# Three lanes on one core: row norms moved to ScalarE, FP4 rescales to GpSimd, two banks for the scan's B rows, and 1,876 unread identity products on TensorE

## The reference

```
x = x + 0.5 * ffn(layernorm(x))      # FP4 quantize/dequantize in blocks of 16, silu-gated, 352 wide
x = x + mamba(layernorm(x))          # 2 layers; each: rmsnorm, in_proj, conv of 4 taps, silu,
                                     # selective scan over 16 states, gate, out_proj
x = x + 0.5 * ffn(layernorm(x))      # the same FP4 ffn
x = x + 0.5 * moe(layernorm(x))      # 8 dense experts 128 -> 512 -> 128, sigmoid gates over 0.5
x = x + attention(layernorm(x))      # its own inner layernorm, 16 heads of 8, relative bias, causal
x = x + 0.5 * moe(layernorm(x))
```

## Time and profile before

| | before |
|---|---|
| median of 3 runs | 2972.98 us (2966.27 to 2973.26) |
| the profiled execution: its time, its span | 2990.37 us, 2988.6 us |
| TensorE busy | 2550.3 us (85%) |
| VectorE busy | 2134.1 us (71%) |
| ScalarE busy | 1498.5 us (50%) |
| GpSimd busy | 1255.3 us (42%) |
| mean granted TensorE clock | 0.836 of full speed |

### The profile page before, as it was taken

How to read it: one execution, slowest core, us unless ns; L and a number is a source line. 1 busy time by engine, 2 the same in 40 slices (tenths; PEclk the granted TensorE clock), 3 DMA queues, 4 the chain that set the end, 5 groups by cost and what they waited for, 6 DMA issues and landing times.

```text
span 2988.6 us, 34443 instructions
## 1 busy us (share of the span) xinstructions
PE 2550.3 (85%) x11161; PEld 1535.6 (51%) x11161; DVE 2134.1 (71%) x4265; ACT 1498.5 (50%) x2989; POOL 1255.3 (42%) x1050
## 2 busy tenths in 40 slices
PE   3667656886899797998999899979899999999898
PEld 2121122443357553665557565746566566567675
DVE  6878899889885778557586988788786866652420
ACT  1432332543374453545466447655665557456554
POOL 1537546473653154352442554535272454510111
PEclk9565566896696896679988899979899999899899
DMA  4213212121221011210110112111020112100000
GB/s 141 78 53 95 73 58 79 49 81 49 64 78 36 19 56 48 60 54 19 52 52 29 58 32 67 47 54 60 26 89 24 45 54 65 50 4 1 1 4 4
DMA packets 88544, 150.12 MB, mean 50 GB/s; under 512 B 10565, under 2 KB 21485, under 8 KB 88110
## 3 DMA queue, kind: packets, MB, share of 16 engines
q1 hardware_dynamic: 88366, 147.94, 15.9%
HBM read 145.26 MB, written 2.65 MB: 49 GB/s over the span
## 4 chain that ended last, share of the span: by engine, by line
PE 65%; DVE 23%; ACT 6%; issue 4%; POOL 2%; DVEq 0%; DMA 0%; SPq 0%; POOLq 0%; ACTq 0%
PE c_bank L861 16%; PE c_bank L869 16%; DVE hst L658 8%; PE a_bank L709 6%; DVE a_bank L652 4%; PE b_bank L1023 4%; PE a_bank L699 3%; PE b_bank L1012 3%; PE b_bank L1036 2%; PE b_bank L1035 2%; PE a_bank L680 2%; PE b_bank L539 1%; PE b_bank L520 1%; PE b_bank L1034 1%; PE a_bank L715 1%
## 5 line engine op out<-in xcount | busy, mean ns | idle before, releaser
L778 POOL TENSOR_TENSOR prod_c<-hst,prod_c 128x512 f32<-128x512 f32 x512 | 662.6, 1295 | 716.7 <-DVE hst L658 710.7
L658 DVE TENSOR_TENSOR_SCAN hst<-dA,a_bank 128x512 f32<-128x512 f32 x512 | 623.4, 1218 | 21.1 <-ACT dA L767 7.9
L861 PE MATMUL c_bank<-c_xT,w 128*128 128x512 f32 x1024 | 565.1, 658 | 15.0 <-ACT hid L893 8.4
L767 ACT ACTIVATE dA<-delta,a_neg 128x510 f32<-128x510 f32 x512 | 364.6, 718 | 360.5 <-DVE hst L658 355.9
L869 PE MATMUL c_bank<-w,hid 128*128 128x128 f32 x4096 | 537.0, 282 | 0.0
L869 PEld LDWEIGHTS c_bank<-w,hid 128*128 128x128 f32 x4096 | 497.5, 195 | 66.8 <-issue 37.5
L893 ACT ACTIVATE hid<-c_bank,b 128x512 f32<-128x512 f32 x512 | 350.0, 687 | 193.0 <-PE c_bank L861 190.9
L652 DVE TENSOR_TENSOR a_bank<-du,a_bank 128x512 f32<-128x512 f32 x512 | 354.9, 693 | 126.0 <-PE a_bank L699 98.2
L917 POOL TENSOR_TENSOR xs<-xs,weighted_y 128x512 f32<-128x512 f32 x128 | 168.0, 1313 | 643.2 <-ACT weighted_y L901 642.7
L709 PE MATMUL a_bank<-prod_c,ident 128*128 128x512 f32 x512 | 389.0, 851 | 26.8 <-POOL prod_c L783 18.6
L699 PE MATMUL a_bank<-bc,sel 64*128 64x512 bf16 x512 | 244.5, 477 | 170.7 <-DVE a_bank L652 159.6
(11 more groups left out here) (168 smaller groups left out, 3387.1 us busy)
## 6 DMA issues: line engine op xcount, KB each, us to landing
prod_c<-c_rows SPq DMA_DIRECT2D x512, 256.0 KB, 3.2
w<-in_w SPq DMA_DIRECT2D x2, 2048.0 KB
xs<-in_x SPq DMA_DIRECT2D x8, 256.0 KB, 8.2
bias<-skew SPq DMA_DIRECT2D x1, 2048.0 KB, 8.6
out_dram<-xs SPq DMA_DIRECT2D x8, 256.0 KB, 2.3
in_wT<-in_in_wT SPq DMA_DIRECT2D x1, 512.0 KB
c_rows<-bcC SPq DMA_DIRECT2D x16, 32.0 KB, 1.6
b_hq<-in_w_gu SPq DMA_DIRECT2D x1, 384.0 KB, 3.2
```

The source lines that it names most:

```text
L658: nc.vector.tensor_tensor_scan(hst[:, s % RS, :], dA[:, s % RA, :], S.bank[0][:, :], 0.0, ALU.mult, ALU.add).then_inc(M.h.sem, 1)
L767: nc.scalar.activation(half_batches(dA[:, s % RA, :], 1), half_batches(delta[:, h, :], 1), ACT.Exp, scale=a_neg[:, l, h, n:n + 1]).then_in ...
L778: nc.gpsimd.tensor_tensor(prod[:, s % RP, :], hst[:, s % RS, :], cring[:, s % RC, :], ALU.mult).then_inc(M.pp.sem, 1)
L861: nc.tensor.matmul(S.bank[up_bank(e, c)][:, :], w1[:, e, c * 128:(c + 1) * 128], S.xT[:, :], start=True, stop=True).then_inc(M.up.sem, 1)
```

## The change

It has four parts, and the order strings of all engines are new.

1. **Norms.** `normed_dve` is gone. `normed_act` applies every norm on ACT, in four activations of 128x128 with `rstd` as scale and a new `shift` (minus mean times rstd) as bias. POOL makes `shift` in two further 128x4 instructions. The rms norm of a mamba layer takes its squares on ACT (`squares_act`, with an accumulating output) in place of `bn_stats`, `bn_aggr` and two small DVE instructions. The adds `x + hm` and `x + x1` go from DVE to POOL.
2. **Rescale.** In the ffn the last instruction of the quantize chain goes to POOL (`rescale_pool`): per ffn one of 128x512 and two of 128x704.
3. **B rows.** The B row of an even step goes to bank 2, that of an odd step to bank 0; DVE multiplies in place and scans the same bank. The row of step s now waits for the scan of step s-2 in place of the multiply of step s-1.
4. **Identity products.** `warm_pe` (letter `d` in `ORDER_PE`) multiplies the identity by itself, 128x128 in float32, into bank 0 of lane c, which nobody reads. It waits once per gap between passes, until the last weighted output of the pass before has left the bank; while a pass is under way (from its transposes to its last `down` product) the string has no `d`. It holds 1,876 of them: 1,086 ahead of pass 0 (layers 0 to 2 of lane a), 381 between passes 0 and 1, 193 between 1 and 2, and 216 between the others up to pass 13.

```
-        def normed_dve(dve, L, S, x, dst, rstd, done, rms=False):
-            dve.wait_ge(rstd.sem, L.at(rstd, 1))
+        def normed_act(act, L, S, x, dst, rstd, done, rms=False):
+            act.wait_ge(rstd.sem, L.at(rstd, 1))
             for t in range(TT):
                 if rms:
-                    ins = nc.vector.tensor_scalar(dst[:, t, :], x[:, t, :], S.rstd[:, t:t + 1], None, ALU.mult)
+                    ins = nc.scalar.activation(dst[:, t, :], x[:, t, :], ACT.Copy, scale=S.rstd[:, t:t + 1])
                 else:
-                    ins = nc.vector.tensor_scalar(dst[:, t, :], x[:, t, :], S.mv[:, t, 0:1], S.rstd[:, t:t + 1],
-                                                  ALU.subtract, ALU.mult)
+                    ins = nc.scalar.activation(dst[:, t, :], x[:, t, :], ACT.Identity, scale=S.rstd[:, t:t + 1],
+                                               bias=S.shift[:, t:t + 1])
...
+        def rescale_pool(pool, L, dst, n, qs, q, made, rounded, k):
+            nb = n // BLK
+            pool.wait_ge(rounded.sem, L.at(rounded, k))
+            nc.gpsimd.tensor_tensor(dst.rearrange("p (b s) -> p b s", s=BLK), q[0][:, 0:n].rearrange("p (b s) -> p b s", s=BLK),
+                                    qs[:, 0, 0:nb].unsqueeze(2).to_broadcast([128, nb, BLK]), ALU.mult).then_inc(made.sem, 1)
             yield
...
-                if s:
-                    dve.wait_ge(M.h.sem, L.at(M.h, s))
-                nc.vector.tensor_tensor(S.bank[0][:, :], du[:, h, :], S.bank[2][:, :], ALU.mult).then_inc(M.dBx.sem, 1)
+                b_bank = S.bank[2 - s % 2 * 2][:, :]
+                nc.vector.tensor_tensor(b_bank, du[:, h, :], b_bank, ALU.mult).then_inc(M.dBx.sem, 1)
...
-                    if s:
-                        pe.wait_ge(M.dBx.sem, L.at(M.dBx, s))
-                    nc.tensor.matmul(S.bank[2][:, :], sel[64:128, s % NST, :], bc3[64:128, :],
+                    if s == 1:
+                        pe.wait_ge(M.delta.sem, L.at(M.delta, 1))
+                    elif s:
+                        pe.wait_ge(M.h.sem, L.at(M.h, s - 1))
+                    nc.tensor.matmul(S.bank[2 - s % 2 * 2][:, :], sel[64:128, s % NST, :], bc3[64:128, :],
...
+        def warm_pe(pe, L):
+
+            waited = 0
+            pe.wait_ge(s_wf, 16 * len(load_f))
+            while True:
+                assert L.passes is not None
+                if waited < L.passes:
+                    waited = L.passes
+                    pe.wait_ge(moe.wy.sem, moe.wy.per * waited)
+                nc.tensor.matmul(sc_.bank[0][:, 0:128], ident[:, :], ident[:, :], start=True, stop=True)
+                yield
```

More of the change, by code:

```diff
@@ L105, with merge @@
 ORDER_SP = (
-    "a246c2a65caca51ca66ca50ca49c3")
-def merge(order, lanes):
+    "a240caca70c2a76ca50ca58ca33c3")
+def merge(order, lanes, spare=None):
     i = 0
     while i < len(order):
-        lane = lanes[ord(order[i]) - ord("a")]
+        lane = spare if order[i] == "d" else lanes[ord(order[i]) - ord("a")]
         j = i + 1
@@ L341, in __init__ @@
                 self.proj = sig(n + "_out_product", 1, use, uses)
+                self.added = sig(n + "_added", 1, use, uses)
         class MoeS:
@@ L406, in stats_dve @@
                 ins = nc.vector.bn_aggr(S.mv[:, t, :], S.stats[:, t, :])
-                if t == TT - 1 and not rms:
+                if t == TT - 1:
                     ins.then_inc(done.sem, 1)
@@ new lines, in rstd_pool, with squares_act @@
+            yield
+        def squares_act(act, L, S, x, done):
+            for t in range(TT):
+                ins = nc.scalar.activation(S.xn[:, t, :], x[:, t, :], ACT.Square, accum_out=S.mv[:, t, 1:2])
+                if t == TT - 1:
+                    ins.then_inc(done.sem, 1)
+                else:
+                    ins.then_inc(L.sem, L.one())
+                yield
+        def normed_act(act, L, S, x, dst, rstd, done, rms=False):
+            act.wait_ge(rstd.sem, L.at(rstd, 1))
@@ L667, in mamba_dve @@
             nc.vector.tensor_tensor(hm[:, :, :], hm[:, :, :], S.bank[0][:, :].rearrange("p (t d) -> p t d", d=D),
-                                    ALU.add).then_inc(L.sem, L.one())
+                                    ALU.add).then_inc(M.added.sem, 1)
             yield
-            dve.wait_ge(L.sem, L.n)
         def mamba_pe(pe, L, S, M, l):
@@ L830, in moe_pe @@
             N = M.norm
+            L.passes = None
             pe.wait_ge(N.out.sem, L.at(N.out, 1))
@@ L1143, in a_pool @@
                 L.g = g
-                yield from rstd_pool(pool, L, sa, mam_ln[0], mam_ln[1])
+                yield from rstd_pool(pool, L, sa, mam_ln.stats, mam_ln.rstd)
                 for l in range(LAYERS):
                     yield from mamba_pool(pool, L, sa, mam[l], l, g * LAYERS + l)
+                last = mam[LAYERS - 1].added
+                pool.wait_ge(last.sem, L.at(last, 1))
+                nc.gpsimd.tensor_tensor(x_of(g), x_of(g), hm[:, :, :], ALU.add).then_inc(first_done.sem, 1)
+                yield
         def a_sp(sp, L):
@@ L1266, in c_pe @@
                 yield from moe_pe(pe, L, sc_, moe)
+        def warm_pe(pe, L):
[7 more added lines that the diff above has]
+                nc.tensor.matmul(sc_.bank[0][:, 0:128], ident[:, :], ident[:, :], start=True, stop=True)
+                yield
         def c_act(act, L):
             act.wait_ge(s_wc, 16 * len(load_c))
-            for i in range(len(moe_order)):
+            for i, (second, g) in enumerate(moe_order):
                 L.g = i
-                yield from moe_act(act, L, sc_, moe)
+                yield from moe_act(act, L, sc_, moe, x_of(g))
         def c_pool(pool, L):
```

257 lines of the change are left out of this document (147 added, 110 removed).

## The result

The changed kernel takes **2876.5 us**, the median of 4 runs (2874.22 to 2881.22), against 2973.12 for the kernel before (4 runs, 2966.27 to 2989.48). The ratio is 0.9669, 95% interval 0.9624 to 0.9714. The forecast was 2847 us with a range of 2740 to 2965. On a second chip and with more runs the ratio was 0.9692 (0.9651 to 0.9734). The traced execution of the kernel before (2990 us) lies 17 us above its median here and 34 above that on the chip of the first experiments, so stretches read from it are about 1% long.

What follows compares the result with a forecast made beforehand. DVE's scans were taken to bound the kernel from 60 to 420 us and PE from 1184 us on, with both mattering between. 678 + 1854 + 92 + 240 = 2864 us of span, scaled to 2847 us, range 2740 to 2965.

Steps and rivals of the forecast that it cites:

- Place one: Start of layer 3 in lane a, where pass 0's first `up` product stands in the new order: 422 us.
- 20 + 133 = 153 us: PE's work at full speed up to 420 us in the kernel before, to which 244 us of identity products were added.
- The 25 us of idle time: PE idle time added up to the start of layer 3, since PE can't start before its first weights are quantized.
- Place two: Near the start of layer 5, where pass 1's first `up` product stands: 678 us, from 150 work, 86 products, 20 idle.
- The rest: From layer 5 to the end: 1854 us of work, 92 of identity products, 240 of overhead.
- open term: How much of some 320 us of overhead inside the passes goes; 110 us idle and 130 by the clock were taken to stay.
- main case: Gaps filled and overhead inside the passes down to 240 us: 2864 us of span, 2847 scaled; chance 0.40.
- first rival: Only the gaps are filled, idle time and clock inside the passes stay at 320 us: 2944, 2927 scaled; chance 0.27.
- three reasons: For less overhead inside the passes: two banks for the B row, some 170 us off DVE, passes entered at full clock.
- The scaling: The 2864 us span was lowered to 2847 because the profiled execution was 0.6% over the median.
- the clock does not rise: Rival: identity products don't raise the clock and cost 0.45 us each: some 3330 us; chance 0.03.
- Lane a gains nothing, but lane c is ahead: At layer 5 lane a stands as now, while pass 0 begins some 110 us earlier and pass 1 about 100.

Runs made afterwards that it cites:

- no_d: The changed kernel with all identity products taken out of PE's order: 2928.5 us, 0.9908 of the kernel before.
- late_d: The changed kernel with only the 409 identity products behind pass 1 kept: 2882.9 us, 0.9747 of the kernel before.
- half_d: The changed kernel with every second identity product left out over the whole order, 938 kept: 2851.7 us, 0.9641 of the kernel before.
- half_early: The changed kernel with 734 of the 1,467 identity products up to pass 1 kept, and all 409 behind it: 2866.5 us, 0.9633 of the kernel before.
- d32: The changed kernel with all 1,876 identity products cut from 128 to 32 columns: 3331.6 us, 1.119 of the kernel before.

## Why the prediction was right, step by step

**Place one.** 422 predicted, 436 measured. By the rows the changed kernel does 415.49 x 0.99 = 411 us of work up to layer 3 and no_d 259.18 x 0.66 = 171. Both need a correction that the prediction's "20 + 133 = 153 us" needs too. The row of the first 60 us gives a clock of 1.00, but the records there have the length of the lower level, and the clock rises only in the second of these (kernel before):

```profile
56.65 2.77 PE L539 MATMUL b_bank<-w_dnT,ffn_buf 128*128 128x128 f32 x12
...
59.85 1.82 PE L539 MATMUL b_bank<-w_dnT,ffn_buf 128*128 128x128 f32 x12
```

Twelve records of the same product take 1.50 us at the full clock (L582 at 55.73 us, changed kernel). So the first 20 us of busy time are about 10 of work, and the prediction's 153 was 143. With the same correction (the lower level up to 21 us in the changed kernel, up to 51 in no_d) the two kernels do 408 and 163 us of work. The difference over 1,086 products is 0.226 us each, priced at 0.225: the price held. The 25 us of idle time came out as 28 (20 idle, 8 by the clock). Mis-sized was the other work: 163 us, not 153. no_d has 548 records ahead of that place where the kernel before has 468; 24 of the 80 more are the transposes and gate products of pass 0, the other 56 products of the ffn in lane b, which now also stand ahead of it.

**Place two.** 678 predicted, 694 measured, of which 14 are from place one. Between the two 258 us were measured, 256 predicted.

**The rest.** 1854 + 92 = 1946 us of work predicted; 2066.91 x 0.94 = 1943 measured. Overhead 240 predicted, "110 us idle and 130 by the clock"; measured 114 and 124. This open term, which separated the main case from the first rival, came out as taken. Against the kernel before it fell by some 220 us. By the table of passes and gaps the fall has the parts that the prediction gave it. The gaps gave up 87 us of idle time and 52 of the clock's, where 86 and 55 stood; the passes 5 and 67, where 10 and 70 stood. The fall in the gaps is the products': no_d loses as much in them as the kernel before (266 and 262 us). The fall in the passes is not, since no_d has it too. So of the three reasons that the prediction gave for it the third, that PE enters each pass at the full clock, is not seen: the clock takes 60 us of the passes in no_d and 53 in late_d. Two banks and the lighter DVE are left, with the new order; the runs don't separate them.

What was wrong are the amounts that this was to be taken from. The prediction had 141 us in the gaps, all of them to go, and 320 inside the passes. Counted from the first `up` product to the last `down` product, the passes held 164 and the gaps 262, and 123 of these are still there. The two errors cancel in the sum, and that they do is luck. (From no_d to late_d the products give back 41 us of idle time and 104 of the clock's, another split than that against the kernel before: no_d has less idle time in the gaps, 116 us in place of 158, and loses more there by the clock, 150 in place of 104.)

**The scaling.** The span was 2864 predicted and 2875 measured. I scaled it down by 0.6%, because the profiled execution of the kernel before was that much above its median. The changed kernel's profiled execution was at its median (2876.84 against 2876.5). 17 of the 29 us between 2847 and 2876.5 are this step.

**What the text said would show.** L912 at about 430 and 690 us: 439 and 696. Busy times near 1960, 1630, 1380: 1946, 1606, 1371. The clock above 0.95 up to the first pass: 0.99; near 0.9 later: 0.94. L1338 was busy 483 us, where 420 stood: its records overlap, and it was the spacing that was priced. Pass 3, where the prediction found a stretch at 0.50 with PE busy throughout, still has one:

```profile
1175.00:1200.00 25.00, 25.00 (x68) 14.14 (x66) 12.15 (x29) 11.59 (x24) 10.90 (x10) 0.50 0.17 53
```

The whole pass has a clock of 0.89 in the changed kernel (1077 to 1235 us) and in no_d (1104 to 1262), and 0.77 before (1184 to 1375): the products did not mend it. The activations of the norms took 0.483 us, not 0.368, and the wide rescales on POOL 1.416, not 1.78.

**A reading.** Against "the clock does not rise" the prediction set L709's 2.07 us for two records beside its mean of 0.85 for one. A single record of L709 takes 1.06 to 1.22 us at the lower level and 0.59 at the full one, so a mean of 0.85 puts about half of its run at the full clock, not most. The conclusion stands: the records of L709 had both lengths.

**What was not foreseen.** "Lane a gains nothing, but lane c is ahead" was taken as if the earlier start were a gain of itself, and no_d shows it isn't much of one: 0.9908 with it, 0.9909 for two banks without it. That DVE's wait for the B row would rise: it is 128.8 us in no_d as well and 99.4 with two banks alone, so it comes with the new order or the moved work and not with the products. The work off DVE had no price of its own, only a share in the open term; the rescales alone turned out to be worth about 1% (0.9811 against 0.9692 by ratio, 2903 against 2885 us by median, on two chips). And half the products would do: half_d and half_early are the fastest kernels measured.

Not tried: the norms back on DVE, and a single bank in the new order. Their shares within no_d's 0.9% stay open.

## What to carry to other kernels

Unread products pay only as a trade that must be added up for each stretch: TensorE's idle time and clock loss that they remove, against 0.225 us each. Between the passes, where DVE's and ACT's chains leave TensorE idle and a stretch of TensorE-bound work follows, 99 us of them returned 145. In the scans, which DVE paces as long as no products stand in them, 337 returned 341 and half as many returned 218 for 193, and on the old order the same idea cost 2.8%. In the passes, where none stood, the clock's loss did not change. Try half the density before believing in the full one, and a kernel without any before giving them the credit.

## What the runs showed of the hardware

- TensorE at 299.46 of 300 us busy had a mean granted clock of 0.55 with 32-column float32 products, and 0.94 at 324.79 of 422 us busy with half as many of 128 columns (half_early). The clock does not follow the busy share.
- A float32 product of the identity, each with its own weight load, took 0.425 us with 32 columns and 0.426 with 128 at the lower clock, and 0.208 and 0.222 at the full one (d32 and the changed kernel). A quarter of the columns saved 6% at most; the clock made a factor of two.
- TensorE was busy 25.00 of 25 us at a granted clock of 0.50 inside pass 3 of the changed kernel, as it was for 46 us before. Products in the gaps did not reach it.
- Some 100 late products left the clock at 0.89 and the third stretch at 2237 us, with some 200 it was 2181 at 0.93, the same as with 409 at 0.94.
- The granted clock of a stretch at the very start reads 1.00 while the records have the length of the lower level: three of 128 columns took 0.90 us there (11.25 us, kernel before) and 0.49 at 2868.
